# Halving the pieces of side work that TensorE takes on between scan steps

## The reference

```
h  = layernorm(x) * (1 + scale) + shift            # scale, shift from the conditioning
xz = h @ in_w ; xs, z = split(xz) ; xs = silu(xs)  # 256 -> 2 x 512
proj = xs @ xproj_w                                # 512 -> 512 (dt) + 64 (B) + 64 (C)
dt = softplus(proj[:512] + dt_bias)
state = state * exp(dt * A) + (dt * xs) * B        # for every position, 512 x 64 states
y = sum over states of state * C ; y = (y + xs * D) * silu(z) @ out_w
```

## Time and profile before

| | |
|---|---|
| median of three runs | 5335.75 us |
| profiled execution | 5332.06 us, its span 5330.4 us |
| VectorE busy | 4722.8 us (89%) |
| TensorE (matmul) busy | 4933.2 us (93%) |
| GpSimd busy | 3750.4 us (70%) |
| ScalarE busy | 3424.6 us (64%) |
| granted TensorE clock | 0.989 mean |

### The profile page before, as it was taken

The page is one execution under the profiler, slowest core; times in us unless marked ns, Lnnn a source line. Parts: engine busy times, 40 slices in busy tenths (PEclk is TensorE's granted clock), DMA queues, the critical chain, the costliest instruction groups (busy, mean ns, idle before and its releaser), DMA issues. The chain is left out here.

```text
span 5330.4 us, 130492 instructions
## 1 busy us (share of the span) xinstructions
PE 4933.2 (93%) x44784; PEld 2525.2 (47%) x44784; DVE 4722.8 (89%) x2419; ACT 3424.6 (64%) x11498; POOL 3750.4 (70%) x6613
## 2 busy tenths in 40 slices
PE   6999999999999999999999999999999999876898
PEld 4444444444444444444445444444445444443444
DVE  2999999999999999999999999999999999996443
ACT  4776767666776767666776767666766767663112
POOL 4787868777786868777786868777786868674211
PEclk8999999999999999999999999999999999998899
DMA  3121111111121211111121211111121211113442
GB/s 106 39 64 43 61 41 53 56 38 61 40 63 43 65 38 53 56 38 61 40 63 42 65 37 54 55 38 61 42 62 38 65 37 44 36 29 106 143 157 67
DMA packets 433144, 306.75 MB, mean 58 GB/s; under 512 B 215920, under 2 KB 336240, under 8 KB 432496
## 3 DMA queue, kind: packets, MB, share of 16 engines
q1 hardware_dynamic: 428272, 294.39, 18.3%
q10 hardware_dynamic: 4224, 4.19, 0.2%
HBM read 187.27 MB, written 111.15 MB: 56 GB/s over the span
## 5 line engine op out<-in xcount | busy, mean ns | idle before, releaser
L891 DVE TENSOR_TENSOR_SCAN b_hs<-b_dA,b_u 128x1024 f32<-128x1024 f32 x2048 | 4537.7, 2269 | 242.5 <-ACT b_u L818 147.9
L1056 PE MATMUL b_ex<-b_dd,b_aw 32*128 32x512 f32 x8192 | 2651.2, 641 | 27.4 <-POOL b_dd L534 15.4
L1043 PE MATMUL b_u<-b_ud,b_bw 32*128 32x256 f32 x16384 | 2322.0, 400 | 262.3 <-DVE b_hs L891 249.5
L800 ACT ACTIVATE b_dA<-b_ex 128x496 f32<-128x496 f32 x4096 | 2291.2, 590 | 151.2 <-PE b_ex L1056 134.4
L1043 PEld LDWEIGHTS b_u<-b_ud,b_bw 32*128 32x128 f32 x16384 | 1434.8, 184 | 1121.7 <-issue 652.6
L1075 PE MATMUL b_y<-b_hs,b_cw 128*32 128x256 f32 x16384 | 1308.9, 390 | 2.3 <-DVE b_hs L891 2.3
L534 POOL TENSOR_TENSOR b_dd<-b_dr,b_mask 128x512 f32<-128x512 f32 x1024 | 1073.3, 1048 | 52.8 <-DVE b_hs L891 39.9
L543 POOL TENSOR_TENSOR b_ud<-b_ur,b_mask 128x512 f32<-128x512 f32 x1024 | 1083.5, 1058 | 0.0
L818 ACT ACTIVATE b_u<-b_hin 128x32 f32<-128x32 f32 x1792 | 365.9, 204 | 1098.6 <-PE b_u L1043 867.7
L1056 PEld LDWEIGHTS b_ex<-b_dd,b_aw 32*128 32x128 f32 x8192 | 831.7, 183 | 76.3 <-ACT b_dA L800 41.1
L570 POOL TENSOR_TENSOR b_hm<-b_first,b_hs 128x32 f32<-128x32 f32 x1792 | 479.8, 268 | 508.8 <-ACT b_first L799 487.7
(11 more groups left out here) (104 smaller groups left out, 2273.6 us busy)
## 6 DMA issues: line engine op xcount, KB each, us to landing
b_u<-scratch_ut SPq DMA_DIRECT2D x256, 128.0 KB, 2.9
scratch_y<-b_ysb SPq DMA_DIRECT2D x128, 256.0 KB, 2.3
scratch_xs<-b_xs SPq DMA_DIRECT2D x64, 256.0 KB, 2.4
scratch_sz<-b_sd SPq DMA_DIRECT2D x64, 256.0 KB, 2.2
scratch_dt<-b_sd SPq DMA_DIRECT2D x64, 256.0 KB, 2.1
scratch_ut<-b_uT SPq DMA_DIRECT2D x64, 256.0 KB, 2.4
b_ur<-scratch_ut SPq DMA_DIRECT2D x1024, 16.0 KB
b_dr<-scratch_dt SPq DMA_DIRECT2D x1024, 16.0 KB, 1.7
```

The source lines that it names most:

```text
L800: nc.scalar.activation(dA[:, j % NDA, h, :, 1:TC], src[:, :, 1:TC], ACT.Exp).then_inc(exp_done, 1)
L891: nc.vector.tensor_tensor_scan(hs[:, v, :, :, kp].rearrange("p d t -> p (d t)"), dA[:, j % NDA, :, :, :].rearrange("p h d t -> p (h d t)") ...
L1043: ins = nc.tensor.matmul(dst[:, :, tb, :], bw[row(r), c % 2, tb, :], ud[row(r), j // 2 % NPR, tb, :, :], start=(tb == 0), stop=(tb == NTB ...
L1056: nc.tensor.matmul(e[bank_of[what]][:, :], aw[row(r), p % DIRS, v, :, :].rearrange("p b s -> p (b s)"), dd[row(r), (p * PAIRS + j // 2) % ...
```

## The change

Each product of two or four matmuls in one or two steps becomes one matmul per step, in runs of two (`project_xz`) or four steps (`project_dt`, `project_bc`); the transposes go two per step over two steps. The start slots stay as they were. The spans in `job_slots` grow accordingly (1 to 2 for xz, 3 to 4 for dt, 4 to 5 for bc, 1 to 2 for the transposes of inputs and B, 1 to 3 for those of x), so `share_banks` gives the banks otherwise. ScalarE takes every result one step later. On GpSimd the first five `times_sigmoid` stay in their slots, the softplus parts and `times_sigmoid` 5 and 6 move one step later, and the last stays.

```diff
-        BC_SLOT, BC_SPAN = (35, 51), 4
-        DT_SPAN = 3
+        BC_SLOT = (35, 51)
+        XZ_SPAN, DT_SPAN, BC_SPAN, UT_SPAN, TURN_SPAN = 2, 4, 5, 2, 3
...
-                    at[XZ_SLOT[i][b]] = (base + XZ_JOB[i] + b, 1)
+                    at[XZ_SLOT[i][b]] = (base + XZ_JOB[i] + b, XZ_SPAN)
...
     (GpSimd's unit)
                         yield from wait_steps(4)
+                    yield
                     for j in range(JB):
...
-                    yield from wait_steps(6)
+                    yield from wait_steps(5)
                     times_sigmoid(q, JB + 3)
...
     (ScalarE's unit)
                     for i in range(JB + 1):
+                        yield
                         take_xz(q, i, 0)
                         yield from wait_steps(2)
                         take_xz(q, i, 1)
                         yield
                         plus_one(q, i)
-                        yield from wait_steps(2)
+                        yield
                     for j in range(JB):
-                        yield from wait_steps(2)
+                        yield from wait_steps(3)
                         take_dt(q, j, 0)
...
     (TensorE)
                     for t in range(TB):
+                        if t == TB // 2:
+                            yield
                         last = nc.tensor.transpose(...)
...
                     for k in range(MB):
+                        if k:
+                            yield
                         last = nc.tensor.matmul(job_bank(n)[:, 0:SEQ], win[:, k, i * P:(i + 1) * P], ...)
...
                     for k in range(JB):
                         ins = nc.tensor.matmul(...)
-                        if k == 1:
-                            yield from wait_steps(gap)
+                        if k + 1 < JB:
+                            yield
...
                     for i in range(JB + 1):
-                        project_xz(q, i, 0)
+                        yield from project_xz(q, i, 0)
+                        yield
+                        yield from project_xz(q, i, 1)
                         yield from wait_steps(2)
-                        project_xz(q, i, 1)
-                        yield from wait_steps(3)
                     for j in range(JB):
                         yield from project_dt(q, j, 0)
-                        yield from wait_steps(3)
+                        yield from wait_steps(2)
                         yield from project_dt(q, j, 1)
-                        yield from wait_steps(3)
+                        yield from wait_steps(2)
```

More of the change, by code:

```diff
@@ L946, in project_xz, with project @@
                     last.then_inc(full, 1)
-                def project(n, cols, b, gap):
+                def project(n, cols, b):
                     bank_free(n)
@@ L1007, in unit @@
[L1007 to L1014, removed]
+                            yield from turn_inputs(q, 0)
+                            yield from wait_steps(2)
+                            yield from turn_b(q)
+                        else:
+                            yield from turn_inputs(q, 1)
+                            yield from wait_steps(2)
+                            yield from turn_inputs(q, 2)
@@ L1015, in unit @@
+                        yield from wait_steps(2)
+                    yield from project_xz(q, JB + 1, 0)
                     yield from wait_steps(2)
-                    project_xz(q, JB + 2, 1)
-                    yield from wait_steps(3)
-                    project_xz(q, JB + 3, 0)
+                    yield from project_xz(q, JB + 1, 1)
+                    yield from wait_steps(4)
+                    yield from turn_inputs(q, 3)
                     yield from wait_steps(2)
-                    project_xz(q, JB + 3, 1)
@@ L1021, in unit @@
-                    yield from wait_steps(5)
+                    yield from project_xz(q, JB + 2, 0)
+                    yield
+                    yield from project_xz(q, JB + 2, 1)
+                    yield from wait_steps(2)
+                    yield from project_xz(q, JB + 3, 0)
+                    yield
+                    yield from project_xz(q, JB + 3, 1)
+                    yield from wait_steps(4)
                     if q % DIRS and q + 1 < PASSES:
                         for k in range(MB):
-                            turn_x(q // DIRS + 1, k)
-                            yield from wait_steps(4)
+                            yield from turn_x(q // DIRS + 1, k)
+                            yield from wait_steps(3)
@@ L1027, in _ @@
                 for k in range(MB):
-                    turn_x(0, k)
+                    for _ in turn_x(0, k):
+                        pass
                 for _ in unit(0):
```

27 lines of the change are left out of this document (14 added, 13 removed).

## The result

Five runs of the changed kernel gave 5360.1 us (median; 5358.5 to 5364.7), five of the kernel before on the same chip 5335.75 (5330.0 to 5338.1). The ratio is 1.0052, 95% interval 1.0041 to 1.0063: **slower, by 24 us, where 7 us faster was forecast, and outside the range of 5285 to 5353.** The profiled execution's span is 5356.8 us, 26.4 longer than before, at a granted clock of .99 as before.

A forecast was written before the change was run, and what follows sets the result against it. VectorE's scans (2.178 us each) were taken to set the time, side work costing 307 us on top. +.31 in 15 passes (+4.7) and -11.5 at the turns gave -6.8: 5335.75 to 5329 us, range 5285 to 5353.

The forecast's parts named there:

- the first price: Step length on TensorE: 1.65 us without side work, plus .53 per side matmul, free up to 2.178.
- the same walk: Arithmetic carrying four step prices through all 128 steps in each engine's issue order; forecast -6.8 us; chance .52.
- so the margin there stays: GpSimd, middle of a pass: softplus and its logarithms move one step together, so the carries lose no margin.
- Rival C: TensorE: handing the array over costs time at added side runs, 43 us bound, 5351; sign, lone matmul over .58; chance .09.
- rival B: GpSimd's carry later than walked at 14 places a pass, 5350; sign, L818's wait on L575 past twice; chance .15.
- Banks.: Longer-held banks make exponents wait: .44 after a step of 2.18, second-exponent bank reused 84 times a pass instead of 53.
- The other sign: Scan gaps of .8 to 1.0 at steps 28, 44, 60 and 76 would be roughly halved.
- GpSimd's six places: Sigmoids 0 to 4 and 7 lose a step of margin: stretch 16 to 25 +1.55, 100 to 112 +1.06 a pass.
- Rival A: GpSimd's carries all in time: 85 us less lost, 5244; half of it likelier, 5285 to 5300; chance .24.
- Turn: Steps 112 to 128 of seven turning passes: halved transposes cut the loss from 1.75 to .10, -11.5 us in all.
- steps 100 to 112: End of a pass: loss goes from 1.61 to 2.67, +1.06 a pass, from GpSimd's late carries.
- Steps 0 to 16: Start of a pass, xz runs: loss falls by .50 a pass.

The follow-up runs named there:

- experiment 7: Kernel before with each xz product's two matmuls either side of L1075: 5425.4 us, against 5388.6 us for a control with all side work ahead of L1075.
- experiment 1: Changed kernel with GpSimd's sigmoid multiplies 0 to 4 and 7 also one step later: 5327.5 us, ratio .9987 to the kernel before.
- experiments 11 and 10: GpSimd's softplus, sigmoids 5 to 7 and norms one step later: in the kernel before, 5301.0 us (11); in the kernel of experiment 5, 5254.6 us (10).
- Experiment 12: Changed kernel with experiment 1's later sigmoids, plus softplus parts, sigmoids 5 to 7 and norms one step later again: 5259.4 us, ratio .9862.
- experiment 8: Kernel before with only the xz products halved and taken a step later, GpSimd's sigmoids also a step later: 5339.9 us, ratio 1.0015.
- experiment 5: Changed kernel with xz products whole and their takes and all sigmoids as before; dt, bc and transposes stay in pieces: 5318.6 us, ratio .9972.
- the fastest: Kernel of experiment 5 with GpSimd's softplus parts, sigmoids 5 to 7 and norms one step later: 5254.6 us, ratio .9854.

## Why the prediction was wrong

- **The first step that failed is the first price, "so .53 each"**: the length of a step with one side matmul. I divided the 1.06 of two by two. Steps of one last 1.65 + .63 = 2.28, not the 2.18 that "is just what a scan takes", so every run of halves falls behind by .10 a step before any bank wait. With .63 in the same walk the sum is +29 instead of -7, against +24 in the medians and +26 in the spans. Steps 25 to 57 come out at +.17 and 57 to 89 at -.33, where -.85 and -.81 stood and +.20 and -.03 were seen: four fifths of what failed to come there. The .63 is measured, and experiment 7 shows that an added handover costs time; that share of four fifths is the walk's, as no run has a lone matmul of .53.
- **The second is "so the margin there stays"**, of the carries in the middle of a pass. The softplus waits for its logarithm hardly longer than before, 180.2 us against
```profile
POOL b_ey L479 <- ACT b_wy L686: 163.8, 64, 6.9
```
in the kernel before, but the carry behind it is now what ScalarE waits for: with the six places of experiment 1 put right, L818's wait for the carry is still 365.0 us against 228.4 before. And with that wait gone the forecast gains come: 1.21 and .85 between experiments 11 and 10, where .85 and .81 were forecast, although a lone matmul is .63 there too. In time, GpSimd's step alone is worth 32 us, these halves alone 16, both together 79. So the gain of the halves was there in steps 25 to 89 and stood behind GpSimd's queue. With the carries late, the walk loses the gain to the .63; with the carries early, the runs have it in spite of the .63. How much of the 24 us belongs to which, the runs do not say.
- My own rows held the answer. The earlier trace rows give 1.06 for 1024 columns; the earlier trace rows .66 for 512, less the same tail of .07, .59 (two records of a matmul are 2 x 256 columns, four transposes 4 x 128). Had it been all columns, it would have been .53. The line through the two leaves .12 that no column pays for and makes a lone matmul .59; the lone ones then showed .20 and .63.
- Rival C had the right kind of mechanism and the wrong size. I bounded the handover by the tail of .07, which overlaps the next step in every run, long or short (and the .70 records above against steps of .63). Its sign, "a single side matmul taking over .58 (C)", came true. The Trainium skill's drain of about 128 cycles ("TensorE: Matmul & The Clock Gate", section "Step-by-step: what each phase is for"; an estimate of .05 us) does not reach it either: by it a lone one would be .58, and .63 was measured. The sign of rival B came true as well: L818's wait on L575 grew from 228.4 to 484.5 us, "past twice", though the one carry followed above came only .06 later than walked.
- *Banks.* The mechanism is there and large: 113 us alone, where 112 were expected. The sign I had named failed: L1070 waits on L804 in 95 places, not "far more than 128". A step of 2.28 leaves only 2.62 - 2.28 = .34 of the wait, and the injects run beside it; it shows as steps of 2.55 and not as idle time: the second exponent of a pair starts later, under the first's record, so L1070's records cover 2727.9 us against 2651.2, though one of them lasts .64 on the average in both kernels. The other sign held: the gaps at steps 28, 44, 60 and 76 went from .95, .95, .95 and .54 to .53, .29, .32 and .51 (medians over the passes).
- *GpSimd's six places.* Right in place and near in size: +1.77 and +1.03 where +1.55 and +1.06 were forecast; giving the margin back is worth 33 us. Rival A priced the carries at 85 us for a kernel in which all are in time, 5244; I had listed eight carries of the middle of the pass as last and left them there. Experiment 12, all the halves with GpSimd a step later, is the nearest to it: 5259.4, 15 above that 5244 and 101 us below the changed kernel.
- *Turn* and *steps 100 to 112*: as forecast in the pass shown. *Steps 0 to 16*: half of the gain was missing, and this half was GpSimd's: with the sigmoids' margin back (experiment 1) they gain 1.96 - 1.47 = .49, the forecast's .50, with the halves and the .63 as they were.

What stays open: how the 24 us divide between the two steps; why halved xz cost 8 us and not 14 in experiment 8, and the 5 us by which the walk was low in experiment 5. And what makes up the .20 inside TensorE was not tried apart; the experiments show when it is paid, not by which part.

## What to carry to other kernels

A piece of work put between others has a fixed price besides its columns; read it from two sizes, or from a lone one, before it is cut smaller, and never by dividing a merged row by its count. When TensorE's idle places are worth filling more evenly, look first at which in-order queue stands before a dependent piece with something urgent behind it: here one step of margin on GpSimd was worth 32 us without the halves and 64 with them, the best halves without it 16. A change that seems worthless may be hidden behind such a queue: the same halves gave 16 us with the carries late and 46 with them early (5301.0 to 5254.6). And a buffer that is reserved longer is paid by whoever rotates through what is left, here with 113 us.

## What the runs showed that I had not expected

- Going from the tiled matmuls (32*128 and 128*32 in the rows) to 128*128 side matmuls and back costs .20 us (.63 for one matmul, 1.06 for two), and it is paid in full also where the products of y follow (experiment 7). Short pieces pay most of it too: two transposes take .37 and four .59, which leaves .37 - .22 = .15. The next inject after two transposes, in the changed kernel:
```profile
1773.55 0.44 PE L993 MATMUL b_ex<-b_ident,b_us 128*128 128x128 f32 x2
1773.92 0.48 PE L1057 MATMUL b_u<-b_ud,b_bw 32*128 32x256 f32 x2
```
- TensorE's busy share in a stretch says little of its load: in steps 25 to 57 the same 689 records cover 77.19 us in the changed kernel, 76.78 in that of experiment 5 and 75.60 in the fastest, always just under the width of the stretch. The records are no longer: an inject's lasts .40, an exponent's .64 and one of the products of y .39 on the average in all of them. They overlap, and where one starts late under another the same records cover more, so short waits do not show as idle time.
